# Two gated forms of the coupling output: made by GpSimd from normalized tokens and broadcast rows, or by matmuls with diagonal gates

## The reference, cut to what matters

```
h  = layernorm(x) * (1 + scale) + shift
x0 = h
for cycle in 3:                      # x <- x + c * twist(x), in effect, c from a small network on x
    per token strength = f(net(x), global(x0))
    x = x + strength * twist(x)
out = residual + gate' * x_after_3_cycles
twist([o_r, o_i, p_r, p_i]) = [p_r, -p_i, -o_r, o_i]
```

```
out = residual + alpha * (gate' * x0) + beta * (gate' * twist(x0))
```

## Time and profile before

| | us |
|---|---|
| median of 3 runs | 1179.05 (1177.37 to 1180.38) |
| profiled execution, span from first to last instruction | 1175.3 |
| TensorE matmul busy | 1067.3 (91%) |
| VectorE busy | 734.6 (63%) |
| ScalarE busy | 596.7 (51%) |
| GpSimd busy | 467.8 (40%) |

### The profile page before, as it was taken

The page is one execution under the profiler, slowest core; times in us unless marked ns, Lnnn a source line. Parts: engine busy times, 40 slices in busy tenths (PEclk is TensorE's granted clock), DMA queues, the critical chain, the costliest instruction groups (busy, mean ns, idle before and its releaser), DMA issues. The chain is left out here.

```text
span 1175.3 us, 19800 instructions
## 1 busy us (share of the span) xinstructions
PE 1067.3 (91%) x6630; PEld 603.4 (51%) x6630; DVE 734.6 (63%) x1549; ACT 596.7 (51%) x1133; POOL 467.8 (40%) x692
## 2 busy tenths in 40 slices
PE   5699999999999998479999974899999998999997
PEld 3244455454454443336565642566666665455654
DVE  2867878787787783624332322767787874566756
ACT  3167667676767666113332322443444442876752
POOL 2444635444453511068888874323333420000000
PEclk9599999999999999579999996999999998999999
DMA  4531414233250411436766672021210002001001
GB/s 150 99 58 18 87 37 89 65 70 82 52 105 21 73 40 47 155 103 138 162 162 135 138 154 71 6 65 42 76 39 26 35 15 95 1 10 63 28 28 54
DMA packets 73540, 85.05 MB, mean 72 GB/s; under 512 B 12560, under 2 KB 67800, under 8 KB 73312
## 3 DMA queue, kind: packets, MB, share of 16 engines
q1 hardware_dynamic: 61088, 66.99, 21.9%
q0 software_dynamic: 12288, 16.79, 8.4%
q10 hardware_dynamic: 64, 0.02, 0.0%
HBM read 45.31 MB, written 25.21 MB: 60 GB/s over the span
## 5 line engine op out<-in xcount | busy, mean ns | idle before, releaser
L566 DVE TENSOR_REDUCE nmax<-psum 128x1 f32<-128x512 f32 (+3 forms) x352 | 215.6, 637 | 44.6 <-PE psum L790 39.8
L683 ACT ACTIVATE pT<-psum 128x512 f32<-128x512 f32 x320 | 181.2, 596 | 65.5 <-PE psum L811 35.5
L788 PE MATMUL psum<-k6T,q6T 96*128 96x512 bf16 (+3 forms) x512 | 128.7, 312 | 15.2 <-DVE nmax L566 11.3
L808 PE MATMUL psum<-q6T,k6T 99*128 99x512 bf16 x320 | 119.3, 382 | 1.1 <-ACT pT L683 0.9
L1093 POOL DMA_INDIRECT residual<-expert_y,idx_e x64 | 101.3, 1583 | 25.2 <-issue 17.1
L1612 DVE TENSOR_TENSOR l_scores<-psum,const_sb 128x512 f32<-128x512 f32 x128 | 79.5, 684 | 19.1 <-PE psum L1787 19.0
L788 PEld LDWEIGHTS psum<-k6T,q6T 96*128 96x128 bf16 x512 | 46.0, 100 | 88.4 <-DVE nmax L566 55.2
L790 PE MATMUL psum<-negs_bf,ident_bf 128*128 128x128 bf16 (+2 forms) x352 | 89.0, 253 | 0.0
L823 PE MATMUL psum<-pT,v 128*32 128x512 f32 x640 | 85.0, 604 | 0.0
L1080 POOL DMA_INDIRECT expert_tokens<-router_input,idx_e x64 | 63.2, 987 | 50.0 <-POOLq L913 30.8
L1745 PE MATMUL psum<-l_hT,l_w 128*128 128x512 f32 x128 | 66.4, 643 | 1.6 <-ACT l_hT L1680 0.9
(11 more groups left out here) (298 smaller groups left out, 2245.4 us busy)
## 6 DMA issues: line engine op xcount, KB each, us to landing
q6T<-q_parts SPq DMA_DIRECT2D x96, 128.0 KB, 4.3
expert_w<-in_ew SPq DMA_DIRECT2D x16, 768.0 KB
x_in<-in_x SPq DMA_DIRECT2D x8, 512.0 KB, 4.2
residual<-x SPq DMA_DIRECT2D x32, 128.0 KB, 1.9
router_input<-h SPq DMA_DIRECT2D x32, 128.0 KB, 1.8
l_x<-residual SPq DMA_DIRECT2D x8, 512.0 KB, 6.6
x_dram<-l_x SPq DMA_DIRECT2D x32, 128.0 KB, 1.7
out<-c_out SPq DMA_DIRECT2D x16, 256.0 KB, 2.1
```

Source lines behind the costliest of these rows:

```text
L566: dve.tensor_reduce(nmax[:, i, u * nh:(u + 1) * nh], ps_s[:, n % SR, 0:nh * (i + 1) * P].rearrange("p (h k) -> p h k", h=nh), AX_X, ALU.ma ...
L683: act.activation(pT[:, n % PR].rearrange("p h t -> p (h t)"), ps_t[:, n % TR, :], ACT.Exp, scale=HD ** -0.5).then_inc(probs, 1)
L788: pe.matmul(out[:, a, :], q6T[0:6 * HD, b % 2, u * nh + a, i * P:(i + 1) * P], k6T[0:6 * HD, b % 2, 0:w], start=a == 0, stop=False, skip_g ...
L808: last = pe.matmul(out, k6T[:, b % 2, j * P:(j + 1) * P], q6T[:, b % 2, hg * 4:hg * 4 + 4, i * P:(i + 1) * P], start=True, stop=j < i)
```

## The change

- The diagonals, the `oT` matmuls, their PSUM banks and the gate columns go. `c_x0T` has two buffers instead of three.
- A new step `uv` at place -199: GpSimd makes, for each pair of token tiles, `u = xn * row0 + row1` and `v = twisted xn * row2 + row3`, from `c_xn` and four rows per batch, broadcast over the partitions. That is five tensor_tensor instructions a pair (three of 128x512, two of 128x256, of which the products come first and the sums wait for them), four pairs a round. It waits for `xn`, for the rows and, from round 2 on, until all of round q-2 is stored, since `oT` now writes its result over `u`. `xn` of the next round waits for uv's products.
- `oT` on VectorE has the same two instructions, with `u` and `v` in SBUF in place of PSUM.
- The rows: in routing TensorE makes shift, scale and gate in row form (8 x 768), ScalarE copies them; in the expert phase, after the first expert, VectorE makes the four products with 13 instructions; SyncE stores them to DRAM, and loads them broadcast to 128 partitions: four loads of 512 KB in the linear phase, two per round for rounds 2 and 3, each after uv of the round before the last is done.

```diff
-MOD_COLS = (0, 1, 2, 3, 6, 7, 8, 9, 10, 11)
+MOD_COLS = (0, 1, 2, 3, 6, 7, 8, 9)
...
+                act.activation(m.cpl.mod_row[:], ps_crow, ACT.Copy)
...
+                for lo, hi in ((0, 2 * C), (2 * C, 3 * C)):
+                    for k in range(KC):
+                        pe.matmul(ps_crow[:, lo:hi], m.silu[:, 1, k, :], wmod[:, k, 3 * C + lo:3 * C + hi],
+                                  start=k == 0, stop=k == KC - 1)
...
-                link(gate(m.modT[:, 1, 10:12, :], ctmp[:, 0], ctmp[:, 1]))
...
+                    if e == 0:
+
+                        shift, scale, g = (m.cpl.mod_row[:, n * C:(n + 1) * C] for n in range(3))
+                        row4 = m.cpl.row4
+                        link(dve.tensor_scalar(scale, scale, 1.0, None, ALU.add))
+                        link(gate(g, rtmp[:, 0], rtmp[:, 1]))
+                        dve.tensor_tensor(row4[:, 0], scale, g, ALU.mult).then_inc(crow_final, 1)
+                        dve.tensor_tensor(row4[:, 1], shift, g, ALU.mult).then_inc(crow_final, 1)
+                        link(dve.tensor_copy(rtmp[:, 0], g))
+                        link(dve.tensor_scalar(rtmp[:, 0, 64:192], rtmp[:, 0, 64:192], -1.0, None, ALU.mult))
+                        for n, v in ((2, scale), (3, shift)):
+                            dve.tensor_tensor(row4[:, n, 0:P], v[:, P:C], rtmp[:, 0, 0:P], ALU.mult)
+                            dve.tensor_tensor(row4[:, n, P:C], v[:, 0:P], rtmp[:, 0, P:C], ALU.mult).then_inc(crow_final, 1)
...
-    "diag": -166,
+    "uv": -199,
...
+def coupling_rows(m, b):
+
+    return m.mod_rows[b:b + 1, ROW_COUPLING * C:(ROW_COUPLING + 4) * C].to_broadcast([P, 4 * C])
...
+                    if s[0] == "uv" and s[1] >= 2:
+                        q = s[1]
+
+                        sp.wait_ge(v_ready, NT * (q - 1))
+                        for a in range(2):
+                            sp.dma_start(rows[:, q % 2, a], coupling_rows(m, 2 * q + a)).then_inc(rows_loaded[q % 2], 16)
...
+                    if s[0] == "uv":
+                        q = s[1]
+                        pool.wait_ge(xn_ready, q + 1)
+                        settle(pool, m.passed)
+                        pool.wait_ge(rows_loaded[q % 2], q // 2 * 32 + 32)
+                        settle(pool, m.passed)
+                        if q >= 2:
+
+                            pool.wait_ge(store[q % 2], 16 * NT * (q // 2))
+                            settle(pool, m.passed)
+                        for n in range(0, 2 * NT, 2):
+                            by = rows[:, q % 2, n // NT].rearrange("p (r c) -> p r c", r=4)
+                            to_u, to_v = u[:, q % 2, n:n + 2, :], v[:, q % 2, n:n + 2, :]
+                            pool.tensor_tensor(to_u, xn[:, n:n + 2, :], by[:, 0:1, :].to_broadcast([P, 2, C]), ALU.mult).then_inc(uv_steps, 1)
+                            pool.tensor_tensor(to_v[:, :, 0:P], xn[:, n:n + 2, P:C], by[:, 2:3, 0:P].to_broadcast([P, 2, P]), ALU.mult)
+                            pool.tensor_tensor(to_v[:, :, P:C], xn[:, n:n + 2, 0:P], by[:, 2:3, P:C].to_broadcast([P, 2, P]),
+                                               ALU.mult).then_inc(uv_steps, 1)
+                            pool.wait_ge(uv_steps, 2 * (NT * q + n // 2) + 2)
+                            settle(pool, m.passed)
+                            pool.tensor_tensor(to_u, to_u, by[:, 1:2, :].to_broadcast([P, 2, C]), ALU.add).then_inc(u_ready, 1)
+                            pool.tensor_tensor(to_v, to_v, by[:, 3:4, :].to_broadcast([P, 2, C]), ALU.add).then_inc(v_ready, 1)
...
-                        dve.wait_ge(o_fill, o_use[s] + 1)
-                        if q >= 2:
-                            dve.wait_ge(store[q % 2], 16 * NT * (q // 2))
-                        link(dve.scalar_tensor_tensor(out=ot[:, q % 2, n, :], in0=ps_o[:, n % 2, 0:C], scalar=al3[:, i, a:a + 1],
+                        dve.wait_ge(u_ready, NT * q + n // 2 + 1)
+                        dve.wait_ge(v_ready, NT * q + n // 2 + 1)
+                        link(dve.scalar_tensor_tensor(out=u[:, q % 2, n, :], in0=u[:, q % 2, n, :], scalar=al3[:, i, a:a + 1],
...
@@ xn on ScalarE
+                            act.wait_ge(uv_steps, 2 * NT * q)
...
-                    if s[0] == "diag":
...
-                        for w in range(2):
-                            for k in range(KC):
-                                last = pe.matmul(ps_o[:, n % 2, (KC * w + k) * P:(KC * w + k + 1) * P],
-                                                 o[:, q % 3, a, 1 - k if w else k, i * P:(i + 1) * P], diag[:, q % 3, a, KC * w + k, :],
-                                                 start=True, stop=True)
```

More of the change, by code:

```diff
@@ L910, in routing_phase @@
         ps_row = m.psum[0:B, 3, 0:C]
+        ps_crow = m.psum[0:B, 4:6, :].rearrange("b n f -> b (n f)")[:, 0:3 * C]
         tables = sem("route_tables_ready")
@@ L1451, in _ @@
                         sp.dma_start(nxt.x_in[:], m.x3_d[0:2 * NT].rearrange("i p c -> p i c")).then_inc(nxt.in_loaded[0], 16)
+                        sp.wait_ge(nxt.row_stored, 16)
+                        for q in range(2):
+                            for a in range(2):
+                                sp.dma_start(nxt.rows[:, q, a], coupling_rows(m, 2 * q + a)).then_inc(nxt.rows_loaded[q], 16)
             @block.gpsimd
@@ L1864, in coupling_steps @@
 def coupling_steps():
-    steps = [("ln",), ("st",), ("xn",), ("diag",), ("fin",)]
+    steps = [("ln",), ("st",), ("xn",), ("uv",), ("fin",)]
     steps += [("hT", a, k) for a in range(2) for k in range(KC)] + [("g", n) for n in (1, 2, 3)]
@@ L1899, in coupling_lead @@
     lead.x_in = sb("c_x_first", [P, 2 * NT, C])
-    lead.cols = sb("c_cols", [P, 6, 2])
-    lead.sgate = sb("c_gate_signed", [P, KC, 2])
+    lead.cols = sb("c_cols", [P, 4, 2])
+    lead.mod_row = sb("c_mod_row", [B, 3 * C])
+    lead.row4 = sb("c_row_products", [B, 4, C])
+    lead.rows = sb("c_rows", [P, 2, 2, 4 * C])
+    lead.row_stored = sem("cpl_rows_stored")
+    lead.rows_loaded = [sem(f"cpl_rows_loaded{s}") for s in range(2)]
     lead.bst = sb("c_bst", [P, 2 * NT, 6])
@@ L1940, in coupling_phase @@
         w1, w2, w3, w4, w4pair, g1w, g2w, g3w = lead.w1, lead.w2, lead.w3, lead.w4, lead.w4pair, lead.g1w, lead.g2w, lead.g3w
-        bias, half, mhalf, nsgn, cols, sgate = lead.bias, lead.half, lead.mhalf, lead.nsgn, lead.cols, lead.sgate
+        bias, half, mhalf, cols, rows, rows_loaded = lead.bias, lead.half, lead.mhalf, lead.cols, lead.rows, lead.rows_loaded
         bst, mv, rstd, vtmp, nbias, xn = lead.bst, lead.mv, lead.rstd, lead.vtmp, lead.nbias, lead.xn
@@ L2015, in _ @@
                         sp.dma_start(m.out_t[q * 2 * NT + n - 1:q * 2 * NT + n + 1].rearrange("i p c -> p i c"),
-                                     ot[:, q % 2, n - 1:n + 1]).then_inc(store[q % 2], 16)
+                                     u[:, q % 2, n - 1:n + 1]).then_inc(store[q % 2], 16)
                 for s in range(2):
@@ L2150, in step @@
                         ins.then_inc(xn_ready, 1)
-                    if s[0] == "diag":
-                        q = s[1]
-                        act.wait_ge(cols_ready, q + 1)
-                        if q >= 3:
-                            act.wait_ge(o_fill, 2 * NT * (q - 2))
-                        for a in range(2):
-                            for k in range(KC):
-                                act.activation(diag[:, q % 3, a, k, :], ident, ACT.Copy, scale=cols[:, 4 + k, a:a + 1])
-                                ins = act.activation(diag[:, q % 3, a, KC + k, :], ident, ACT.Copy, scale=sgate[:, k, a:a + 1])
-                        ins.then_inc(diag_ready, 1)
                     if s[0] == "hT":
@@ L2251, in step @@
                         for k in range(KC):
-                            last = pe.matmul(ps_1[:, n % 2, :], w1[:, w, k, h * P:(h + 1) * P], o[:, q % 3, a, k, :],
+                            last = pe.matmul(ps_1[:, n % 2, :], w1[:, w, k, h * P:(h + 1) * P], o[:, q % 2, a, k, :],
                                              start=k == 0, stop=k == KC - 1)
@@ L2288, in step @@
                         last.then_inc(tok_fill, 1)
-                    if s[0] == "oT":
-                        _, q, n = s
-                        a, i = n // NT, n % NT
-                        pe.wait_ge(diag_ready, q + 1)
-                        if o_use[s] >= 2:
-                            pe.wait_ge(done, o_use[s] - 1)
-                        for w in range(2):
-                            for k in range(KC):
-                                last = pe.matmul(ps_o[:, n % 2, (KC * w + k) * P:(KC * w + k + 1) * P],
-                                                 o[:, q % 3, a, 1 - k if w else k, i * P:(i + 1) * P], diag[:, q % 3, a, KC * w + k, :],
-                                                 start=True, stop=True)
-                        last.then_inc(o_fill, 1)
                 for s in order:
```

45 lines of the change are left out of this document (19 added, 26 removed).

## The result

The changed kernel takes 1209.26 us (median of 4, 1208.63 to 1213.42), the kernel before beside it 1179.38 (4 runs, 1177.37 to 1180.38): ratio 1.0269, 95% interval 1.0251 to 1.0287, slower by 29.9 us by the medians and 31.7 by the ratio. The forecast was 1207. The profiled execution is the one of 1213.42, span 1211.3, 36.0 above the span before, so some 6 us of what follows belong to the two profiled executions and not to the change.

The account below looks back on a forecast made before the run. TensorE, busy throughout from the coupling phase's second round, seemed to bound the kernel, but some of its matmuls only filled waits. On the 1179.05 us median, -11.9 + 15 + 8 + 10 + 3 + 3.8 = +27.9 gave 1207, range 1192 to 1219.

Parts of the forecast that it names:

- matmuls and diagonals gone: Coupling phase: 4.2 us gained in each of second and third rounds, 2.1 in the tail, 1.4 in last tiles; together 11.9.
- wait at xn(3): Fourth normalization waits for GpSimd, whose uv(2) must wait for the store of round 0; 15 us lost, bounds 10 and 17.
- lock, first round: Coupling phase, first round: VectorE's instructions with two SBUF inputs wait out GpSimd's; 8 us lost, between 4.3 and 12.2.
- lock, tail: End of coupling phase: 14.4 us of uv(3) remain where VectorE has no rest; 10 us lost, between 6 and 13.4.
- clock: Coupling phase: TensorE works at half clock after two or three long gaps; 3 us lost, 0 to 6.
- routing: TensorE's added row-form passes, 5.6 us less 1.7 for dropped columns, delay the index transposes; 3.8 us lost.
- row store and loads: Row store and four 512 KB loads run beside the linear phase on a waiting queue; nothing lost, 0.5 us at most.
- the prediction's own rule: Range ends set two thirds of the way to the sums of low ends, +10 us, and high ends, +41.
- the part for VectorE in uv's way: Within the wait at xn(3): VectorE's collisions with uv(2) add another 4 to 5 us to the 10.8 of queue wait.
- My bounds: First-round lock: 12.2 us late if each VectorE two-input instruction waits for one of uv's, 4.3 if one in two.
- Lock-free with the queue alone: Rival for the coupling phase: no lock between instructions of this size, only GpSimd's queue; +3.7 us, 1183; chance 0.12.
- The forecast's signs: GpSimd some 85 us busier, VectorE's products far above 0.69 us, ScalarE idle over 10 us, index transposes some 4 later.

Follow-up runs that it names:

- uv_small: As rows_late, but each of GpSimd's products and sums cut to 8 columns of its two tiles, all waits kept; 1169.11 us, ratio 0.9920.
- rows_late: The changed kernel with the four 512 KB broadcast loads put behind the last output tile of batch 6 of the linear phase; 1202.13 us, ratio 1.0200.
- writes_clean: As rows_late, but GpSimd's uv instructions are fills that read nothing, 640 columns in round 0 and 1024 in the others; 1179.26 us, ratio 1.0037.
- only_round1: GpSimd makes the gated forms of round 1 alone; the other rounds keep diagonals and gate matmuls as before the change; 1183.29 us, ratio 1.0071.
- before_loads: The kernel before, with only four unused 512 KB broadcast loads added where the changed kernel issues its own; 1183.95 us, ratio 1.0075.
- experiment 4: Two kernels on rows_late with GpSimd's uv replaced by fills that read nothing: 1190.45 us, ratio 1.0098; with shorter round 0 fills (writes_clean) 1179.26, ratio 1.0037.
- Experiment 7: As rows_late, but GpSimd's 128x512 instructions cut into two of 128x256 each, 32 a round instead of 20; 1199.96 us, ratio 1.0213.
- only_round0: GpSimd makes the gated forms of round 0 alone; rounds 1 to 3 keep diagonals and gate matmuls as before the change; 1174.54 us, ratio 1.0002.

## Why the prediction was right, and where it was not

Its steps, with what each was worth (differences of ratios at 1178.2 us, or stretches, as named above):

| step | predicted | measured | from |
|---|---|---|---|
| matmuls and diagonals gone | -11.9 | -9.4 | uv_small |
| wait at xn(3) | +15 | +12.4 | wait after; 10.2 without the lock |
| lock, first round | +8 | +9.0 | rows_late less writes_clean |
| lock, tail | +10 | +10.0 | rows_late less uv_small; 9.1 less writes_clean |
| clock | +3 | +2.2 | third stretch, writes_clean less uv_small |
| routing | +3.8 | -0.1 to +0.3 | first pass to index transposes 10.36 before, 10.29 after, 10.66 in rows_late |
| row store and loads | 0 | +7.1 | rows_late, by the medians; 8.1 by the ratios |

The measured column adds up to +31.2 to +31.6; the medians differ by 29.9, and the ratio makes 31.7. The forecast of +27.9 is close to that in part by luck: misses of +7.1 and +2.5 stand against -3.8 and -2.6. The mechanisms of the three large terms, the queue, the lock and the lost matmuls, came out as said. The range was wider than the prediction's own rule made it: two thirds of the way to both ends is 1195 to 1216, not 1192 to 1219. (A smaller slip: 20.4 for uv without its waits should be 20.6. Neither bears on the forecast.)

*Matmuls gone.* The method, comparing a round with tiles to one without, gave 4.2 for the second round, which uv_small confirms at 4.24. Only in the third did it give twice the 2.1 that were there: that round repeats the second in the rows, but in both kernels that have no tiles there and no stall before it, uv_small and only_round1, the clock fell behind the normalization (0.87 over 8.3 us in uv_small) and the stretch took 34.47. The tail's 2.1 and the last tiles' 1.4 came as 2.0 and 1.4. The first stretch, on which I had said nothing, lost 0.46 against before_loads, the price of three tiles in the earlier trace rows; the 1.2 that uv_small has above the kept trace of before is a clock that before_loads has too. The clock term looked at long gaps only.

*uv and its queue.* Round 0 took 21.1 us for the predicted 21.4, and hid. The estimate by the GPSIMD Engine Reference of the Trainium skill, "Performance versus the Vector engine", 18.0 us, was short; the row decided rightly. uv(2) began 2.54 us behind the last tile, as priced. Without the lock xn(3) waited 10.2, predicted 10.8; the fills that stand for uv there are 1.2 shorter than its products. Too large was the part for VectorE in uv's way, 4 to 5: uv(2) took 21.8 us, 0.7 more than round 0 undisturbed. VectorE does work beside it (busy 12.10 of 12.40 us from 1108.40), but there it was mostly VectorE that waited (0.83 to 1.56 us for an output instruction of 0.48), and the normalization does not wait for VectorE.

*The lock.* Mechanism and sizes stand: experiment 4 takes away the reads, and 19.2 us go. The mechanism was too narrow in one point: single-input VectorE instructions wait as well, and do so in part even beside fills. My bounds, one GpSimd instruction for every VectorE instruction or for every second, bracket it. Experiment 7 limits the picture: the price isn't proportional to the piece.

*Routing.* A size from the slower clock. The step named that case ("2 if the clock rises") and still put the floor at 2; it priced the added passes at 5.6 us, which took 4.01, and left the 32 others at their price, though these got cheaper from 0.22 to 0.12 us each (0.16 in rows_late).

*Row loads.* This is the step of the sum that failed outright: "on a queue that waits there anyway: nothing, 0.5 at most". The queue did wait there, but behind it stood batch 5's row, which VectorE had waited 2.7 us for already. So little of the loads' time was covered: the wait grew by 6.4 us. The wait stood in the trace of before; I had asked what the queue waits for, not who waits for the queue.

*The rivals.* Lock-free with the queue alone was put at 1183; writes_clean, which is that case but for the early row loads, is 1182.6 by ratio. The forecast's signs came: products above 0.69 (0.74 to 0.94 in the mean), ScalarE idle 12.39, xn(3) 54.3 us behind xn(2), GpSimd 92 us more busy in the phase; the one of the index transposes did not.

Open: why the clock of the first stretch is 1.00 in the kept trace of the kernel before and 0.86 to 0.93 behind the normalization in before_loads, uv_small and only_round0, although before_loads does the same work there; and why only_round0's runs show nothing of the gain that its profile has (they spread over 7.9 us). Three buffers of gated forms, which would free uv(2) from the store, were not tried, nor was a GpSimd queue with the coefficients first and the gated forms away from VectorE's updates.

## What to carry to other kernels

Work moved to GpSimd is not free when it reads SBUF beside a VectorE that sets the pace: price it on VectorE's path by GpSimd's own time inside that stretch. Here 21 us of it cost 9 where VectorE had some slack, and 14 cost 9 to 10 in the tail, where it had nearly none. Before a load is added to a queue, look at who waits for the next transfer on it; where the trace has a wait there, count the added transfer nearly whole (6.4 us of wait for four loads here). A gap that opens on TensorE costs twice, once as the gap (10 to 12 us) and once as half clock behind it (2.2 us). And before a microsecond or two in one stretch is put down to a change, look at the same stretch in a run that leaves it untouched: here the clock alone moved it by 1.7.

## What the hardware showed that was not expected

- Under contention GpSimd is slowed too, if less than VectorE: in the first stretch it was busy for 31.6 us, coefficients included, where the second, nearly without collisions, has 23.9; VectorE's busy time in the first is 13.1 us above uv_small's (24.4 to 37.5).
- Single-input VectorE instructions wait as well: the tensor_scalar of 128x512 takes 0.543 us in the mean before, 0.770 beside GpSimd's products (up to 1.49) and 0.631 in the phase with fills.
- Small VectorE instructions beside GpSimd's alternate in this trace: 1.21, 0.15, 1.13, 0.15, 1.12, 0.15 us for work of 0.16. Only every second one waits.
- Cutting GpSimd's instructions to half brought nothing (ratio 1.0213 against 1.0200): a round of them takes 22.8 us undisturbed instead of 21.1, and GpSimd is busy 33.7 us in the first stretch instead of 31.6.
- Four row loads of 512 KB delayed a load of 128 KB behind them to 10.8 us from issue to landing, where the same load took 6.5 before and others of its kind 4.0 to 4.8.
- In the routing eight more passes of TensorE ahead of 32 narrow ones cost nothing: the granted clock was 0.61 in the mean over 475 to 505 us (0.56 in rows_late), where it had been 0.50.
